# Transposes of P, scores and value products in one row on TensorE, and key and query roots refined by ScalarE and GpSimd, in a fused attention kernel

## The reference

```
qkv = x @ Wqkv;  q, k, v = split(qkv, 3), 16 heads of 64
q = q / max(norm(q), 1e-12) * qs;   k = k / max(norm(k), 1e-12) * ksc
q = q*cos*scale + rotate_half(q)*sin*scale;   k the same with 1/scale
sim  = 8 * q . k            # 4 windows of 32 queries against 64 keys
attn = softmax(mask(sim));  y = (attn @ v) @ Wo
xn = (y - mean) / sqrt(var + 1e-5) * g + b
a, gate = split(xn @ W1 + b1);  x = a * gelu(gate) @ W2 + b2
```

## Time and profile before

| what | value |
|---|---|
| median of 3 runs | 3191.79 us (3190.32 to 3195.16) |
| the profiled execution | 3188.57 us, its span 3186.8 us |
| TensorE busy | 3060.7 us, 96% of the span |
| VectorE busy | 3035.9 us, 95% |
| ScalarE busy | 2736.0 us, 86% |
| GpSimd busy | 2455.6 us, 77% |
| granted TensorE clock | 0.985 of full |

### The profile page before, as it was taken

How to read it: one execution, slowest core, us unless ns; L and a number is a source line. 1 busy time by engine, 2 the same in 40 slices (tenths; PEclk the granted TensorE clock), 3 DMA queues, 4 the chain that set the end, 5 groups by cost and what they waited for, 6 DMA issues and landing times.

```text
span 3186.8 us, 169111 instructions
## 1 busy us (share of the span) xinstructions
PE 3060.7 (96%) x71268; PEld 2192.5 (69%) x71268; DVE 3035.9 (95%) x6045; ACT 2736.0 (86%) x5443; POOL 2455.6 (77%) x2675
## 2 busy tenths in 40 slices
PE   6777899999999999999999999999999999999997
PEld 4444567777777777777777777777777777777775
DVE  7887899999999999999999999999999999999995
ACT  6887688888888888888888888888888888888885
POOL 3333778888888888888888888888888888888884
PEclk9898999999999999999999999999999999999998
DMA  3000222223222222222222222222222222222222
GB/s 82 7 7 6 53 53 55 58 51 83 66 61 52 57 57 73 75 52 61 52 58 77 66 61 52 61 52 80 69 53 60 52 61 80 67 54 54 59 52 60
DMA packets 151238, 182.24 MB, mean 57 GB/s; under 512 B 51668, under 2 KB 74258, under 8 KB 151186
## 3 DMA queue, kind: packets, MB, share of 16 engines
q1 hardware_dynamic: 151186, 181.55, 21.9%
HBM read 21.32 MB, written 2.10 MB: 7 GB/s over the span
## 4 chain that ended last, share of the span: by engine, by line
PE 90%; issue 3%; DVE 3%; POOL 2%; SPq 1%; ACT 0%; DMA 0%; DVEq 0%; POOLq 0%; ACTq 0%
PE bank L1414 11%; PE bank L1371 9%; PE bank L1342 8%; PE bank L1442 7%; PE bank L1351 6%; PE bank L1306 5%; PE bank L1383 5%; PE bank L1459 5%; PE bank L1424 5%; PE bank L1391 5%; PE bank L1404 5%; PE bank L1450 5%; PE bank L1397 4%; PE bank L1320 4%; PE bank L1334 2%
## 5 line engine op out<-in xcount | busy, mean ns | idle before, releaser
L1414 PEld LDWEIGHTS bank<-wo,oT 128*128 128x128 f32 x3072 | 373.4, 192 | 91.6 <-issue 90.1
L1075 DVE TENSOR_REDUCE sm<-sq 128x32 f32<-128x2048 f32 x192 | 436.3, 2272 | 0.0
L1414 PE MATMUL bank<-wo,oT 128*128 128x128 f32 x3072 | 374.6, 275 | 0.7 <-ACT gl L779 0.7
L539 POOL TENSOR_TENSOR qk<-qk,rn 128x512 f32<-128x512 f32 x192 | 200.2, 1042 | 209.8 <-DVE rn L1032 209.8
L1371 PEld LDWEIGHTS bank<-PT,vs 64*64 64x64 f32 x18432 | 289.1, 135 | 92.6 <-issue 91.8
L584 POOL TENSOR_TENSOR P<-P,rowsum 128x512 f32<-128x512 f32 x192 | 200.1, 1042 | 152.9 <-DVE rowsum L1110 152.9
L1371 PE MATMUL bank<-PT,vs 64*64 64x32 f32 (+1 forms) x18432 | 311.2, 220 | 2.6 <-issue 2.3
L1442 PEld LDWEIGHTS bank<-cst,qk 32*128 32x128 f32 x12288 | 206.8, 137 | 147.7 <-issue 147.4
L1342 PEld LDWEIGHTS bank<-qkT 64*32 64x32 f32 x24576 | 278.2, 105 | 14.2 <-issue 3.9
L1342 PE MATMUL bank<-qkT 64*32 64x64 f32 x24576 | 281.5, 225 | 3.6 <-issue 3.6
L596 POOL TENSOR_TENSOR qk<-ta,tb 128x512 f32<-128x512 f32 x192 | 245.4, 1278 | 8.9 <-DVE tb L1120 8.9
(11 more groups left out here) (164 smaller groups left out, 9313.4 us busy)
## 6 DMA issues: line engine op xcount, KB each, us to landing
vs<-vt SPq DMA_DIRECT2D x1152, 128.0 KB, 2.4
wqkv<-L_ffn_Wqkv SPq DMA_DIRECT2D x18, 512.0 KB, 3.7
zm<-zm SPq DMA_DIRECT2D x192, 31.8 KB
wo<-L_ffn_Wo SPq DMA_DIRECT2D x6, 512.0 KB, 4.9
z_sb<-x SPq DMA_DIRECT2D x4, 512.0 KB, 5.6
ctxb<-ctx SPq DMA_DIRECT2D x32, 64.0 KB, 1.8
w<-L_ffn_W SPq DMA_DIRECT2D x6, 341.0 KB, 3.2
out<-x_sb SPq DMA_DIRECT2D x7, 256.0 KB, 2.7
```

Of the source, the lines that this page charges most:

```text
L1075: v_.tensor_reduce(sm[:, :], sq[:, :].rearrange("p (h d) -> p h d", d=DH), AX.X, ALU.add).then_inc(s["d_sumsq"], 1)
L1414: ins = t_.matmul(bank[7][:, 384:512], oT[:, c, :], wo[:, 2 * (c % 4) + c // 4, :], start=c == 0, stop=c == PAIRS - 1)
```

## The change

TensorE: mask and scores, and then the value products, follow the transposes of P with nothing between. The 512-column product and the transpose of `zn` that stood between them move away. The transposes of q and k go to the head of the slot and to lag 2 (from 1), the last feed-forward product to lag 5 (from 4). VectorE: the statistics of `zm` move from the end of a slot to the head of the next (lag 4 from 3), `z_sb` too (lag 5 from 4). The clamp becomes a maximum by reduction over pairs: `sm` has a second column that holds the floor. The refinement, now n2 = 3 - sc * rn * rn and rn * n2 with a factor 0.5 put into the rotary constants, is a Square and an Identity on ScalarE and two products on GpSimd. The steps of all engines stand in a new order, the loop begins at slot 8 (from 6), and the loads of the next layer stand at other places of SyncE's list. The core of the diff:

```diff
-    c[:, C_ROT:C_ROT + 256] *= np.float32(LN_UP ** 0.5)
+    c[:, C_ROT:C_ROT + 256] *= np.float32(0.5 * LN_UP ** 0.5)
...
-        sm = sb("sm", [128, 2 * HEADS])
+        sm = sb("sm", [128, 2 * HEADS, 2])
+        sc = sb("sc", [128, 2 * HEADS])
...
-        LOOP0, UNROLL = 6, 2
+        LOOP0, UNROLL = 8, 2
...
+            g.memset(sm[:, :, 1:2], LN_UP * NORM_MIN2).then_inc(s["u_sm"], 1)
+            g.memset(three[:, :], 3.0).then_inc(s["u_three"], 1)
...
+                    g.tensor_tensor(n1[:, :], sc[:, :], n0[:, :], ALU.mult).then_inc(s["g_n1"], 1)
...
+                    g.tensor_tensor(rn[:, p, :], rn[:, p, :], n2[:, :], ALU.mult).then_inc(s["g_rn"], 1)
...
-                    a_.activation(lns[:, :], sm[:, :], ACT.Ln, scale=LN_UP).then_inc(s["a_ln"], 1)
+                    a_.activation(lns[:, :], sc[:, :], ACT.Ln).then_inc(s["a_ln"], 1)
...
+                    a_.activation(n0[:, :], rn[:, p, :], ACT.Square).then_inc(s["a_r2"], 1)
...
+                    a_.activation(n2[:, :], n1[:, :], ACT.Identity, scale=-1.0, bias=three[:, 0:1]).then_inc(s["a_n2"], 1)
...
-                    v_.scalar_tensor_tensor(sm[:, :], sm[:, :], NORM_MIN2, sm[:, :], ALU.max, ALU.max).then_inc(s["d_nr0"], 1)
+                    v_.tensor_reduce(sc[:, :], sm[:, :, :], AX.X, ALU.max).then_inc(s["d_nr0"], 1)
...
-                    v_.scalar_tensor_tensor(n0[:, :], sm[:, :], -0.5 * LN_UP, rn[:, p, :], ALU.mult, ALU.mult).then_inc(s["d_nr1"], 1)
...
-                    v_.scalar_tensor_tensor(n1[:, :], n0[:, :], 1.0, rn[:, p, :], ALU.mult, ALU.mult).then_inc(s["d_nr2"], 1)
...
-                    v_.scalar_tensor_tensor(rn[:, p, :], n1[:, :], 1.5, rn[:, p, :], ALU.add, ALU.mult).then_inc(s["d_rn"], 1)
```

SyncE's list at the change of a layer, before and after:

```diff
                 shift_z(end - 6, 0)
+                shift_v(end - 4, 0)
+                shift_z(end - 5, 1)
                 shift_v(end - 3, 1)
-                shift_z(end - 5, 1)
                 if not last:
                     load_qk(layer + 1, 0)
                     load_qk(layer + 1, 1)
+                    load_rot(layer + 1)
+                    load_v(layer + 1)
+                shift_z(end - 4, 0)
                 shift_v(end - 2, 0)
```

More of the change, by code:

```diff
@@ L447, in _ @@
                     load_o(layer + 1)
-                    shift_v(end + 2, 0)
-                    load_b2(layer + 1)
+                if not last:
+                    shift_v(end + 1, 1)
             store(6, 9)
@@ L587, in slot @@
[L587 to L596 removed]
+                    edge(pool, u, "g_add0", done(u))
@@ L1158, in slot @@
                                      .to_broadcast([128, 8, 2, 32]), ALU.mult).then_inc(s["d_rot1"], 1)
-                u, on, p = unit(n, k, 3)
-                if on:
-                    wait(dve, "d_agg", done(u))
-                    v_.tensor_scalar(ve[:, p:p + 1], mv[:, 1:2], LN_EPS, None, ALU.add).then_inc(s["d_ve"], 1)
                 if isinstance(n, int) and UNITS <= n < UNITS + 4:
@@ L1301, in slot @@
+                u, on, p = unit(n, k, 5)
+                if on:
+                    edge(pe, u, "d_h", done(u))
+                    wait(pe, "l_w2", 32 * layer_of(u) + 32)
+                    for j, (_, m_) in enumerate(FCH):
+                        ins = t_.matmul(bank[6][:, 384:512], hT[0:m_, j, :], w2[0:m_, j, :], start=j == 0, stop=j == 2)
+                    ins.then_inc(s["p_y2"], 1)
                 u, on, p = unit(n, k, 0)
                 if on:
-                    wait(pe, "d_rot0", done(u))
@@ L1304, in slot @@
                     edge(pe, u, "a_zs", done(u))
+                    edge(pe, u, "d_rot0", done(u))
                     wait(pe, "l_wk", 16 * layer_of(u) + 16)
                     t_.matmul(bank[0][:, :], zsT[:, p, :], wqkv[:, 1024:1536], start=True, stop=True).then_inc(s["p_qk2"], 1)
+                u, on, p = unit(n, k, 0)
+                if on:
+                    wait(pe, "d_rot1", done(u))
+                    edge(pe, u, "a_zs", done(u))
+                    t_.matmul(bank[1][:, :], zsT[:, p, :], wqkv[:, 1536:2048], start=True, stop=True).then_inc(s["p_qk3"], 1)
@@ L1345, in slot @@
                     ins.then_inc(s["p_S"], 1)
-                u, on, p = unit(n, k, 0)
-                if on:
-                    wait(pe, "d_rot1", done(u))
-                    edge(pe, u, "a_zs", done(u))
-                    t_.matmul(bank[1][:, :], zsT[:, p, :], wqkv[:, 1536:2048], start=True, stop=True).then_inc(s["p_qk3"], 1)
-                u, on, p = unit(n, k, 4)
-                if on:
-                    wait(pe, "d_zn", done(u))
-                    edge(pe, u, "z_ready", done(u - 1) + B if not (isinstance(u, int) and u - 1 < 0) else 0)
-                    t_.transpose(bank[6][:, 0:128], zn[:, :], ident).then_inc(s["p_znT"], 1)
                 u, on, p = unit(n, k, 3)
@@ L1378, in slot @@
                 if on:
-                    wait(pe, "a_zn", done(u))
-                    edge(pe, u, "a_zs", done(u + 5))
-                    wait(pe, "l_w1", 16 * layer_of(u) + 16)
-                    for j, (o, m_) in enumerate(FCH):
-                        ins = t_.matmul(bank[7][0:m_, 128 * j:128 * j + 128], w1[:, FF + o:FF + o + m_], znT[:, :], start=True, stop=True)
-                    ins.then_inc(s["p_gate"], 1)
+                    wait(pe, "d_zn", done(u))
+                    edge(pe, u, "z_ready", done(u - 1) + B if not (isinstance(u, int) and u - 1 < 0) else 0)
+                    t_.transpose(bank[6][:, 0:128], zn[:, :], ident).then_inc(s["p_znT"], 1)
                 u, on, p = unit(n, k, 0)
@@ L1394, in slot @@
                 if on:
+                    wait(pe, "a_zn", done(u))
+                    edge(pe, u, "a_zs", done(u + 5))
+                    wait(pe, "l_w1", 16 * layer_of(u) + 16)
+                    for j, (o, m_) in enumerate(FCH):
+                        ins = t_.matmul(bank[7][0:m_, 128 * j:128 * j + 128], w1[:, FF + o:FF + o + m_], znT[:, :], start=True, stop=True)
+                    ins.then_inc(s["p_gate"], 1)
+                u, on, p = unit(n, k, 4)
+                if on:
                     edge(pe, u, "a_zn", done(u))
```

448 lines of the change are left out of this document (229 added, 219 removed), and 9 rows, old and new, of the table names.

## The result

| | before | after |
|---|---|---|
| time, median of the runs beside each other | 3193.47 us (3190.32 to 3195.43) | 3215.04 us (3210.79 to 3220.6) |
| ratio after to before | | 1.0074, 95% interval 1.0061 to 1.0088 |
| profiled execution, time and span | 3188.57, 3186.8 | 3210.79, 3209.0 |
| start of the first slot | 301.5 | 305.5 |
| first 12 intervals between slots | 174.05 | 177.61 |

The forecast was 3158, in a range of 3148 to 3186. The changed kernel is slower than before instead of faster. A second measurement of it gave 3216.12 and 1.0069 [1.0052, 1.0086]. An interval is the time from one slot's start to the next, read at zcur's transpose; a slot is named by its start.

What follows compares the result with a forecast made beforehand. TensorE's gapless row of matmuls, 14.66 us a slot, was taken as the bound. 182 x 0.197 = 35.9, plus 1 for the fill, minus 4 for the tail, made 33 us less: 3158, range 3148 to 3186.

Steps and rivals of the forecast that it cites:

- Step 1: TensorE's order: tiled groups in one row save one way out and one in, 0.197 us a slot, 14.66 to 14.46.
- rival A: TensorE: the step between the two tiled shapes costs 0.10 like any other; slot 14.56, time 3177; chance 0.13.
- If TensorE stays without holes: Condition on the 14.46 us slot: TensorE never waits; time 3148 to 3168, chance 0.62.
- Step 2: Roots leave VectorE, freeing some 1.7 us a slot; ScalarE's two 0.22 steps and GpSimd's two 0.25 products fit at no cost.
- Step 3: Chain from zn's transpose through ScalarE and VectorE's last rotation to product L1351: 14.25 us, hidden with 0.2 to spare.
- B: That second chain exceeds TensorE's row, so TensorE waits at L1351's product for the last rotation; 14.58 gives 3180; chance 0.10.
- Rival C: VectorE's zn step meets GpSimd's add, TensorE waits 0.54 every slot; 3254; chance 0.09 including other slower outcomes.
- Step 4: Normalization step at the next slot's head: zm's copy, issued at about 14.3, lands within 3.47; no cost.
- Step 5: Load queue at a layer's change: v copies ahead of next q weights, issued 4.2 us into the slot; free, five times.
- the bad case: At the layer's changes, being wrong by one landing of the loads costs 5 x 3.7 = 18 us.
- Step 6: Ends: one thin slot added behind the last unit, 4 us taken from 0 to 14.5; pipeline fill 1 us less.
- filling and entering the loop: Nine of the 191 intervals between 301.5 and 3100.6, left out of the 182 counted as saving 0.197 us each.

Runs made afterwards that it cites:

- split_exit12: Changed kernel with its loop left 12 slots earlier and, in written-out slots alone, the first value product between scores and value products: 3247.57 us, 1.0162.
- roots_only2: Kernel before with the root change alone (maximum as a reduction, refinement on ScalarE and GpSimd), every other order as before: 3189.74 us, 0.9991.
- before_row: Kernel before with transposes of P, scores and value products in one row, ScalarE's znT copy ahead of the fourth square, other orders kept: 3388.63 us, 1.0618.

## Why the prediction was wrong

- **Step 1, TensorE's order: right, and a little small.** 0.25 saved instead of 0.197, a dense slot of 14.41. The step from 64x32 to 64x64 tiles costs nothing: from scores to value products it is 1.39 in after, 1.40 in the earlier trace rows, and the value products take 1.53 in both. So rival A falls. The rule of the Trainium skill (TensorEngine Tiling (Array Packing), Key Properties) that every change of mode drains TensorE shows no price at this one step. At the others there is one: split_exit12's product of 0.86 costs 1.06.
- **"If TensorE stays without holes": this condition failed,** and it was given 0.62. This is the step that cost the forecast most: 36 us of gain became none. The 0.25 was lost to ScalarE's copies, the gate and the start of the round: 0.08 in one slot, 0.41 in the other, 0.25 on average.
- **Step 2, the roots: durations right, place not counted.** The reduction takes 0.20 (0.21 estimated), ScalarE's steps 0.23 and 0.32 (0.22), GpSimd's 0.26 and 0.25. VectorE falls to 907. "Cost nothing as long as the chains below hold" left the chains of these four steps themselves out.
- **Step 3, what is late next: the wrong chain.** The one that I added up ends at 1527.85 with the last rotation (L1182), 0.49 before TensorE uses it at 1528.34. So B, in its form, falls. The chain through zm, zmb, L617 and L885 to the qkT copies was not added up, nor the one from the first rotation through zm to zcur's transpose. Hops were taken at 0.05 to 0.06; two on this chain are 0.20 (zm to zmb, 1525.27 to 1525.47) and 0.24 (last copy to TensorE, 1529.22 to 1529.46), one is 0.02 (L617 to L885).
- **Rival C: didn't happen.** zn takes 0.49 on average and nobody waits for it. The loss came from the other side.
- **Step 4, zm's copy: right.** It is issued at 1525.30 and VectorE's reader starts at 1528.73, 3.43 later, after 0.49 of waiting that costs nothing.
- **Step 5, the layer's change: nearly right.** The two slots there are 3.9 us longer in all five together, in before 0.9: 3 us instead of 0, far below the 18 of the bad case.
- **Step 6, the ends: the second step that failed.** It took +4 for the tail (what stands behind the last slot's start) and -1 for the fill (the first slots). The tail is 12.3 longer, the fill 3.6. The tail was read as one unit's chain with no term for written-out code. In after's tail a stretch of value products takes up to 3.4, with 1.50 of "issue" in it. Issue stalls of over 0.15 us add up to 12.9 in after's first twelve intervals and 5.3 in before's, 4.4 and 1.6 in the tails. So in the fill they are more than the whole loss, and in the tail 2.8 of the 12.3. The granted clock is at 0.50 for 43.6 us of after's tail and 22.5 of before's, while TensorE mostly waits there for other engines. What makes the other 9.5 us stays open, and the extra slot was not separated: roots_only2 has a tail of 87.0, before_row, with the row but without the extra slot, 98.1. The signs stood in the trace of before: the first slots of its loop and those ahead of it took 14.8 to 16.9, put down to "filling and entering the loop" and left at that.

Sum, against the forecast of 33 us less: 36 from the slots came to 0 (steady slots of 14.66 on average), 3 more at the layers' changes, 8 more in the tail and 4.6 more in the fill than taken, and 4 of drift ahead of the first slot: 55.6, and 33 less 55.6 is -22.6, against the 22.2 by which the profiled executions differ. The terms are read from one execution of each kernel, and by the second profile of after the fill alone would be 5 more.

## What to carry to other kernels

When a slot is to become shorter, add up every chain that crosses engines and ends at the engine that sets the time, with hops of up to 0.24 us as measured here, not the one that looks longest: a slack of 0.2 us in 14.5 is gone with the first small step that stands in the wrong queue. Small tiled matmuls use up instructions fast (224 in 2.9 us here): keep a loop's body small enough to stay loaded, write out as few slots as can be, and where code is written out leave long products between its dense groups.

## What was new on the hardware

- Instructions of TensorE are loaded in pieces of 16 KB. A loop of two slots (1440 instructions) loads nothing, one of four loads 3.2 pieces a slot and is 19% slower than before.
- Written out, a slot costs 0.9 us more in the old order of work and 2.6 in the new, at the same number of loads. Each of the 25 issue stalls of these slots ends 2.3 to 2.9 us after the start of a load.
- After some stalls of 1.6 us and more, though not after others as long, TensorE's granted clock was 0.50 for 3.4 us and the slot some 1.7 us longer.
- A loop's jump on ScalarE, an engine that doesn't set the time, took 0.09 to 0.18 us there (L885 to L742) and showed on TensorE as as much in every slot that has it.
